# The first batch's values: maximum and halves a pass sooner, all 25 pieces placed ahead of the first turned probabilities

## The chip, the core and the metric

The kernel runs on one core of a Trainium2 chip. The metric is the time of one execution on the device in microseconds (us), smaller is better. The core has five engines that work side by side and each through its own list of instructions, in order: TensorE (PE in the rows; PEld is its loading of weights), VectorE (DVE), ScalarE (ACT), GpSimd (POOL) and SyncE (SP, which here only issues transfers). An engine that waits for a semaphore holds up all that stands behind the wait in its list.

## The reference

A transformer block on x of 4 batches of 2048 tokens, 512 wide:

```python
x = x + cross_attention(layernorm(x), ctx_768)       # 16 heads of 32, 77 keys per batch
x = x + moe_ffn(layernorm(x))                        # 8 experts, top 2, capacity 1024 tokens
```

Of the attention, what matters here is the side of the values, of each batch b:

```python
v = (key_value @ Wv + bv)                            # 77 rows of 512, for each of 4 batches
attn = softmax(clip(q @ k.T * scale, -1e4, 1e4))
o = einsum('bhqk,bhkd->bqhd', attn, v)
x = x + o @ Wo + bo
```

Products are made in halves: a float32 number is scaled by a power of two taken from the largest magnitude of its tensor, and cut into two float16 numbers, high and low, and three products of halves stand for one of float32.

## The kernel before

The 8192 tokens are 64 tiles of 128; two tiles are a group. A pass h of the main loop works on many tiles at once, each engine at another step of another tile. The loop begins at h = -7; what comes before it in the code sets up keys, values and weights. The order in each engine's list is written out by hand. In pass h:

- TensorE: `o_mm(h)` (out projection, lines 1094 and 1099), `tx(h+11)` (turns the normed tile, 1002), half of `q_mm` (queries of a group, 1029), `pv_mm` (probabilities by values, 1080), `s_mm(h+7)` (scores, 1052), `t2(h)`, the other half of `q_mm`.
- VectorE: `s_sum(h+5)` (1464) and `s_recip`, `residual(h)` (1486), `tx_lo(h+11)` (1430), the statistics of the tiles that `stats_at(h)` names (1317, 1319), and `score(h+7)`: maximum, limit and difference (1435, 1441, 1447).
- ScalarE: `ln1_apply(h+12)` (706), `s_min(h+6)` (737), `tx_hi(h+11)` (716), `s_exp(h+6)` (745), `r_scale(h+5)` (750), `q_hi` (729, 732), `o_hi`, `p_hi(h+5)` (760).
- POOL: `p_norm(h+5)` (542), `q_lo` (524), `o_lo` (530), `p_lo(h+5)` (548), and small steps of the norms in between. `all_max(n, order)` (567) is a reduce over all partitions; it waits until `order` maxima have been made.
- SP: `p_T(h+4)` (the turned copy of the probabilities, 381), `load_x(h+14)` into one of 3 buffers xt (344), `load_s` of the tiles that VectorE's statistics take in the next pass, into one of 2 buffers xs (356; it waits until the statistics two tiles before are made), stores, and from pass -2 on two placed pieces of a later batch.

The values of all four batches are made in float32 (`vf`, 77 partitions). Their maximum is reduced on VectorE (line 1867) and on POOL (`all_max(2, 4)`), a scale comes of it on VectorE (`scale_of`, lines 1362 to 1371), ScalarE makes the high half (line 899) and VectorE the low half (line 1848), into `vsh`. The product needs them elsewhere: heads lie 77 rows apart and not on chunks of 128, so `values_place(b, k)` (line 391) copies them in 25 pieces a batch into `vb`, each a transfer of its own from SP, of 1 to 77 rows with 64 bytes. `pv_mm` of a batch's first group waits for all 25, and for the turned probabilities of its two tiles.

Before the change, the values' maximum stands at the end of pass -7 on VectorE, `all_max(2, 4)` in pass -6 on POOL, the scale in -6, the high half in -6 behind `q_hi`, the low half in -5, and the pieces in passes -5, -4 and -3 of SP (9, 9 and 7), each time behind that pass's turned probabilities and loads. The same scale step of `wo` (`scale_of(3, ...)`) goes side by side with that of the values.

Of the kernel before, what the change touches and what calls it, by code (L numbers as in the profile page):

```python
# [69 lines left out]
def steps(gen, n):  # L70
    for _ in range(n):
        next(gen, None)


def alternate(*gens):
    gens = list(gens)
    while gens:
        for gen in list(gens):
            try:
                next(gen)  # L80
            except StopIteration:
                gens.remove(gen)
# [3 lines left out]
def xattn_moe(nc, x, ctxT, wq, bq, wk, bk, wv, bv, wo, bo, embT, w1T, w2T, out, xrow):  # L86
    ctx = ExitStack()
    with ctx:
# [250 lines left out]
        def sync(sp):  # L339
# [34 lines left out]
            def p_T(t):  # L374
                if not 0 <= t < T:
                    return
                G, j = divmod(t, TG)
                if G >= 2:
                    sp.wait_ge(S["pv"], 2 * (G - 1))
                sp.wait_ge(S["plo"], t + 1)  # L380
                sp.dma_start_transpose(pT[:, G % 2].rearrange("p a c n -> p (a c) n")[:, :, j * P:(j + 1) * P],
                                       ph[:, t % 2].rearrange("p a n -> p (a n)")).then_inc(S[f"pT{t % 2}"], 16)
# [52 lines left out]
                sp.dma_start(wof[DH * j:DH * (j + 1), :, :], wo_j[j]).then_inc(S["l_wo"], 16)  # L435

            for h in range(-7, T):
                p_T(h + 4)
                if h + 14 >= RT + XT:
                    load_x(h + 14)  # L440
                if h >= 1:
                    load_r(h + 4)
                for t in stats_at(h + 1):
                    load_s(t)
                if -5 <= h < -2:
                    for k in range(9 * (h + 5), 9 * (h + 6)):
                        values_place(0, k)
                if h == -2:
                    sp.wait_ge(S["made"], 5)
                    sp.wait_ge(S["bor"], 1)  # L450
                    for i in range(3):
                        sp.dma_start(bo3[i:i + 1, :], bot[0:1, i, :]).then_inc(S["l_b3"], 16)
                store_x(h)
                store_o(h)
                b, beat = (h + 18) // 16, (h + 18) % 16
                if 1 <= b < B:
                    values_place(b, 2 * beat)
                    values_place(b, 2 * beat + 1)
                if h == 50:
                    load_w(0, 1)  # L460
                if h == 56:
                    load_w(0, 2)
                if h in (22, 38, 54):
                    store_s((h - 22) // 16)
# [12 lines left out]
        def gpsimd(pool):  # L477
# [145 lines left out]
            for h in range(-7, T):  # L623
                G, half = divmod(h, 2)
                Q, part = divmod(h + 9, 2)
                if h == -7:
                    all_max(3, 3)
                if h == -6:
                    all_max(2, 4)
                if h == -3:  # L630
                    bias_rows()
                for b in range(2, len(XB)):
                    if h == seed_at(b) + 1:
                        first = norm_pool(b)
                if h == -5:
                    steps(first, 99)
                if h in (16, 32, 48, 61):
                    second = norm2_pool({16: 0, 32: 1, 48: 2, 61: 3}[h])
                if h == 61:
                    steps(second, 99)  # L640
                p_norm(h + 5)
                steps(first, 4)
                steps(second, 2)
                q_lo(Q, 2 * part)
                steps(first, 3)
                o_lo(G + 1, half)
                q_lo(Q, 2 * part + 1)
                steps(first, 9)
                steps(second, 2)
                p_lo(h + 5)  # L650
# [24 lines left out]
        def scalar(act):  # L675
# [71 lines left out]
            def r_scale(t):  # L747
                if 0 <= t < T:
                    act.wait_ge(S["r"], t + 1)
                    act.activation(rr[:, t % 2, :], rr[:, t % 2, :], ACT.Copy, scale=PSC).then_inc(S["rs"], 1)  # L750
# [131 lines left out]
            for h in range(-7, TAIL):  # L882
                G, half = divmod(h, 2)
                Q, part = divmod(h + 9, 2)
                for H in ones_at(h):
                    ones = onehot(H)
                ln1_apply(h + 12)
                s_min(h + 6)
                tx_hi(h + 11)
                if h in (20, 36, 52):  # L890
                    second_exp((h - 20) // 16)
                s_exp(h + 6)
                steps(ones, 1)
                r_scale(h + 5)
                q_hi(Q, 2 * part)
                if h == -6:
                    act.wait_ge(S["scale"], 4)
                    act.wait_ge(S["lo"], 1)
                    act.activation(flat3(vsh[0:NKV, 0]), flat3(vf[0:NKV, :, :]), ACT.Copy, scale=sv[0:NKV]
                                   ).then_inc(S["hi"], 1)  # L900
                if h == -4:
                    act.wait_ge(S["scale"], 4)
                    act.activation(flat3(woh[:, 0]), flat3(wof[:, :, :]), ACT.Copy, scale=so).then_inc(S["hi"], 1)
                o_hi(G + 1, half)
                t2_copy(h)
                q_hi(Q, 2 * part + 1)
                steps(ones, 1)
                p_hi(h + 5)
# [389 lines left out]
        def vector(dve):  # L1298
# [510 lines left out]
            dve.wait_ge(S["l_wo"], 80)  # L1809
            abs_max(3, flat3(wof[:, :, :])).then_inc(S["amax"], 1)  # L1810
            tx_lo(3)
            route = iter(())
            weights = iter(())

            for h in range(-7, TAIL):
                H = inverted_at(h)
                if h in (16, 32, 48):
                    route = routing({16: 0, 32: 1, 48: 2}[h])
                    steps(route, 1)
                if h in (20, 36, 52):  # L1820
                    route = choice((h - 20) // 16)
                if h in (22, 38, 54):
                    route = ranking((h - 22) // 16)
                    steps(route, 1)
                s_sum(h + 5, 0)
                residual(h)
                if H:
                    add_slots(H)
                s_sum(h + 5, 1)
                for g in ones_at(h):  # L1830
                    value(g)
                if H:
                    next_batch(H[-1])
                steps(route, 4)
                s_recip(h + 5)
                tx_lo(h + 11)
                ln2_stats(h)
                ln2_aggr(h)
                for t in stats_at(h):
                    ln1_stats(t)  # L1840
                for b in range(2, len(XB)):
                    if h == seed_at(b):
                        steps(norm1(b), 9)
                if h == -6:
                    alternate(scale_of(3, 5, 3, 2.0 ** -50), scale_of(2, 4, 4, 2.0 ** -50))
                if h == -5:
                    dve.wait_ge(S["hi"], 3)
                    dve.scalar_tensor_tensor(flat3(vsh[0:NKV, 1]), flat3(vf[0:NKV, :, :]), sv[0:NKV],
                                             flat3(vsh[0:NKV, 0]), ALU.mult, ALU.subtract).then_inc(S["lo"], 1)
                    dve.wait_ge(S["early"], 8)  # L1850
                    dve.tensor_scalar(embm[:, :], bM[:, 0:E], -1.0 / D, None, ALU.mult).then_inc(S["embc"], 1)
                    dve.wait_ge(S["embc"], 1)
                    dve.tensor_tensor(embc[:, :, :], embs[:, :, :], embm[:, :].unsqueeze(1).to_broadcast([P, 4, E]),
                                      ALU.add).then_inc(S["embc"], 1)
                if h == -4:
                    dve.tensor_scalar(co, isv, iso, 1.0 / PSC, ALU.mult, ALU.mult).then_inc(S["fact"], 1)
                    bias_scaled()
                if h == -3:
                    dve.wait_ge(S["hi"], 4)
                    dve.scalar_tensor_tensor(flat3(woh[:, 1]), flat3(wof[:, :, :]), so, flat3(woh[:, 0]), ALU.mult,  # L1860
                                             ALU.subtract).then_inc(S["lo"], 1)
                if h in (19, 21, 23, 35, 37, 39, 51, 53, 55):
                    steps(route, 99)
                score(h + 7)
                if h == -7:
                    dve.wait_ge(S["kvf"], 8)
                    dve.tensor_reduce(scr[0:NKV, 2:3], flat3(vf[0:NKV, :, :]), AX_X, ALU.max,
                                      apply_absolute_value=True).then_inc(S["amax"], 1)

            for h in range(TAIL, T):  # L1870
                H = inverted_at(h)
# [156 lines left out]
```

## Time and profile before

| | us |
|---|---|
| median of 3 runs | 1442.85 |
| lowest, highest | 1439.77, 1443.17 |
| the profiled execution | 1441.63 |
| its span | 1439.9 |

Shares of the span in which the engines were busy: TensorE 91%, VectorE 66%, ScalarE 56%, POOL 50%. The attention's passes fill the span until about 780 us, the experts the rest. A row of a timeline gives the start in us, the length in us, engine, line, operation, out<-in, the shape, a count where several alike are merged, and in brackets how long the engine stood idle before it and what ended that. A length can overlap the next start by about 0.1 us. "issue" in the brackets is idle time for which the profile shows no one waited for.

### The profile page before, as it was taken

To read this page: it belongs to the slowest core of one execution; us is meant where nothing else is said; L and a number is where in the kernel's file an instruction comes from. 1 tells how busy PE (TensorE), PEld (TensorE's weight loads), DVE (VectorE), ACT (ScalarE), POOL (GpSimd) and SP (SyncE) were. 2 spreads that over 40 slices of the span, in tenths; PEclk is the share of its full clock that TensorE was granted. 3 is DMA by queue.
4 is the path that set the end of the run, shared out by engine and by line. 5 is a ranking of instruction groups with operands and counts; after the bars stand their busy time and mean duration, and the time that the engine had idled before them with its cause. 6 is when DMAs were issued, how large, how long until landed. Compare 5 with 4: busy or idle time off the path is not lost.

```text
span 1439.9 us, 30591 instructions
## 1 busy us (share of the span) xinstructions
PE 1315.5 (91%) x12330; PEld 775.1 (54%) x12330; DVE 955.1 (66%) x1808; ACT 812.6 (56%) x1336; POOL 715.2 (50%) x717
## 2 busy tenths in 40 slices
PE   6458999989998999997849999999999999999996
PEld 3336777767676677764527444444444444444442
DVE  8678898889889787887775545444554545455421
ACT  4558888878998899987455514233251514334210
POOL 3187878777777678876423232242514223241301
PEclk9869999999999999999869999999999999999998
DMA  6147898978887786788433564565546455654401
GB/s 197 52 94 197 205 251 211 230 188 192 204 219 171 181 182 168 183 220 202 132 102 111 168 177 146 154 177 133 163 124 180 141 151 168 156 138 123 105 15 44
DMA packets 319575, 228.89 MB, mean 159 GB/s; under 512 B 253305, under 2 KB 253689, under 8 KB 319434
## 3 DMA queue, kind: packets, MB, share of 16 engines
q1 hardware_dynamic: 304074, 176.28, 49.4%
q0 software_dynamic: 15360, 50.66, 11.9%
q8 instruction: 97, 1.59, 0.4%
q14 instruction: 44, 0.36, 0.1%
HBM read 118.98 MB, written 50.86 MB: 118 GB/s over the span
## 4 chain that ended last, share of the span: by engine, by line
PE 72%; DVE 12%; POOL 7%; issue 4%; ACT 2%; SPq 2%; DMA 1%; DVEq 0%; POOLq 0%; ACTq 0%
PE ps L1213 23%; PE ps L1199 23%; PE ps L1099 8%; PE ps L1029 7%; PE ps L1080 3%; PE ps L1116 2%; POOL sd L542 2%; PE ps L1013 2%; PE ps L1052 1%; DVE x L1486 1%; POOL qT L524 1%; DVE sm L1464 1%; POOL ph L548 1%; PE ps L1002 1%; POOL oT L530 1%
## 5 line engine op out<-in xcount | busy, mean ns | idle before, releaser
L1199 PE MATMUL ps<-xT,w1s 128*128 128x512 f16 (+1 forms) x1632 | 336.5, 369 | 1.9 <-DVE xT L1729 1.5
L1213 PE MATMUL ps<-w2s,hT 128*128 128x512 f16 x1536 | 332.8, 379 | 0.0
L849 ACT ACTIVATE hT<-ps 128x512 f16<-128x512 f32 (+1 forms) x136 | 77.8, 572 | 356.0 <-PE ps L1199 356.0
L1199 PEld LDWEIGHTS ps<-xT,w1s 128*128 128x128 f16 x1632 | 160.6, 99 | 175.5 <-issue 1.9
L1213 PEld LDWEIGHTS ps<-w2s,hT 128*128 128x128 f16 x1536 | 150.2, 98 | 181.3
L593 POOL DMA_INDIRECT out_dram<-ys,idx x64 | 71.4, 1116 | 278.7 <-DVE ys L1769 274.5
L542 POOL TENSOR_TENSOR sd<-sd,rr 128x1232 f32<-128x1232 f32 x64 | 143.9, 2248 | 117.0 <-ACT rr L750 116.9
L1029 PE MATMUL ps<-xnT,wqh 128*128 128x256 f16 x1536 | 194.3, 278 | 5.7 <-ACT partq L732 5.5
L1099 PE MATMUL ps<-woh,oT 128*128 128x512 f16 x768 | 180.2, 384 | 3.7 <-POOL oT L530 3.7
L1759 DVE SCALAR_TENSOR_TENSOR hT<-ps,hT 128x512 f16<-128x512 f32 (+1 forms) x136 | 88.6, 658 | 138.5 <-ACT hT L849 138.4
L1769 DVE SCALAR_TENSOR_TENSOR ys<-ps,gs,og 128x512 f32<-128x512 f32 x64 | 48.1, 751 | 189.7 <-PE ps L1213 189.7
L548 POOL TENSOR_TENSOR ph<-sd,ph 128x1232 f16<-128x1232 f32 x64 | 162.2, 2534 | 12.2 <-ACT ph L760 11.4
L1029 PEld LDWEIGHTS ps<-xnT,wqh 128*128 128x128 f16 x1536 | 150.6, 99 | 28.9 <-ACT partq L732 6.3
L1099 PEld LDWEIGHTS ps<-woh,oT 128*128 128x128 f16 x768 | 75.2, 99 | 91.3 <-POOL oT L530 6.9
L1080 PE MATMUL ps<-pT,vb 128*32 128x256 f16 (+1 forms) x2400 | 89.0, 283 | 22.2 <-DMA vb<-vsh 11.0
L524 POOL TENSOR_TENSOR qT<-partq,qT 128x256 f16<-128x256 f32 x128 | 87.9, 688 | 35.9 <-ACT partq L732 20.7
L1447 DVE SCALAR_TENSOR_TENSOR sd<-ps,lim,mx 128x1232 f32<-128x1232 f32 x64 | 96.0, 1501 | 6.4
L1464 DVE TENSOR_REDUCE sm<-sd 128x8 f32<-128x616 f32 x128 | 99.5, 783 | 0.0
L1435 DVE TENSOR_REDUCE ps<-ps 128x16 f32<-128x1232 f32 x64 | 91.2, 1425 | 7.2 <-PE ps L1052 7.2
L1486 DVE SCALAR_TENSOR_TENSOR x<-ps,scr,xr 128x512 f32<-128x512 f32 x64 | 48.0, 750 | 66.8 <-PE ps L1099 66.6
L579 POOL DMA_INDIRECT xg<-xrow_dram,gix x64 | 65.6, 1025 | 48.6 <-DVE gix L1677 28.6
L1080 PEld LDWEIGHTS ps<-pT,vb 128*32 128x32 f16 (+1 forms) x2400 | 67.1, 98 | 39.2 <-issue 35.6
(206 smaller groups left out, 2012.4 us busy)
## 6 DMA issues: line engine op xcount, KB each, us to landing
xr<-x SPq DMA_DIRECT2D x64, 256.0 KB, 3.6
xrow_dram<-x SPq DMA_DIRECT2D x64, 256.0 KB, 3.7
out_dram<-x SPq DMA_DIRECT2D x64, 256.0 KB, 4.2
stage<-w1T SPq DMA_DIRECT2D x8, 2048.0 KB, 9.5
stage<-w2T SPq DMA_DIRECT2D x8, 2048.0 KB, 8.4
xt<-x SPq DMA_DIRECT2D x59, 256.0 KB, 3.2
xs<-x SPq DMA_DIRECT2D x56, 256.0 KB, 4.2
wqf<-wq SPq DMA_DIRECT2D x1, 1024.0 KB, 7.8
```

Of the source, the lines that this page charges most:

```text
L524: pool.tensor_tensor(qT[:, G % 2, 1, g, :], partq[:, g % 2, :], qT[:, G % 2, 0, g, :], ALU.subtract).then_inc(S["qlo"], 1)
L542: pool.tensor_tensor(heads(t), heads(t), rr[:, t % 2, :].unsqueeze(2).to_broadcast([P, HEADS, NKV]), ALU.mult).then_inc(S["pn"], 1)
L548: pool.tensor_tensor(ph[:, t % 2, 1, 0:KALL], sd[:, t % SDB, :], ph[:, t % 2, 0, 0:KALL], ALU.subtract).then_inc(S["plo"], 1)
L1029: ins = pe.matmul(bA[n][:, 0:GW], wqh[:, b, k, g * P:(g + 1) * P], xnT[:, G % 2, 4 * a + k, :], start=(k == 0 and i == 0), stop=(k == 3 an ...
L1080: ins = pe.matmul(bA[n][strip, cols], vb[0:K, b, a, k, strip], pT[0:K, G % 2, d, c, :], start=(i == begins[j]), stop=(i == ends[j]), tile_ ...
L1099: ins = pe.matmul(bA[0][:, :], oT[:, G % 2, a, g, j * P:(j + 1) * P], woh[:, b, g, :], start=False, stop=(g == 3 and i == 2))
L1199: ins = pe.matmul(hb[z][:, 0:wide], w1s[e % 2][:, a, k, ic * P:(ic + 1) * P], xT[:, 4 * b + k, cols], start=(k == 0 and i == 0), stop=(k = ...
L1213: ins = pe.matmul(yb[z][:, :], hT[:, a, k, s * P:(s + 1) * P], w2s[e % 2][:, b, k, :], start=(k == 0 and i == 0), stop=(k == 7 and i == 2))
L1435: dve.tensor_reduce(four(raw), scores, AX_X, ALU.max).then_inc(S["raw"], 1)
L1447: dve.scalar_tensor_tensor(sd[:, t % SDB, :].rearrange("p (g j k) -> p g j k", g=4, j=4), scores, lim[:, 2:3], four(mx[:, t % 2, :]).unsqu ...
L1464: dve.tensor_reduce(sm[:, t % 2, hs], heads(t)[:, hs, :], AX_X, ALU.add).then_inc(S["sm"], 1)
L1759: dve.scalar_tensor_tensor(hT[:, 1, ic, cols], hb[(f - 1) % 4][:, 0:count * P], 0.0, hT[:, 0, ic, cols], ALU.max, ALU.subtract).then_inc(S ...
```

## The change

- VectorE: the maximum of `vf` is made before the loop, right behind `tx_lo(3)`. The two scales are made at the end of pass -7 and not in pass -6, the low half in pass -6 and not in -5.
- POOL: `all_max(2, 4)` stands in pass -7, right behind `all_max(3, 3)`.
- ScalarE: the high half, in pass -6 as before, stands ahead of `r_scale` and the first `q_hi` of the pass.
- SP: all 25 pieces of batch 0 are issued at the start of pass -5, ahead of that pass's loads and of the first turned probabilities.

```diff
             for h in range(-7, T):
+                if h == -5:
+                    for k in range(len(pieces)):
+                        values_place(0, k)
                 p_T(h + 4)
...
-                if -5 <= h < -2:
-                    for k in range(9 * (h + 5), 9 * (h + 6)):
-                        values_place(0, k)
...
                 if h == -7:
                     all_max(3, 3)
-                if h == -6:
                     all_max(2, 4)
...
                 s_exp(h + 6)
-                steps(ones, 1)
-                r_scale(h + 5)
-                q_hi(Q, 2 * part)
                 if h == -6:
                     act.wait_ge(S["scale"], 4)
                     act.wait_ge(S["lo"], 1)
                     act.activation(flat3(vsh[0:NKV, 0]), flat3(vf[0:NKV, :, :]), ACT.Copy, scale=sv[0:NKV]
                                    ).then_inc(S["hi"], 1)
+                steps(ones, 1)
+                r_scale(h + 5)
+                q_hi(Q, 2 * part)
...
             tx_lo(3)
+            dve.wait_ge(S["kvf"], 8)
+            dve.tensor_reduce(scr[0:NKV, 2:3], flat3(vf[0:NKV, :, :]), AX_X, ALU.max,
+                              apply_absolute_value=True).then_inc(S["amax"], 1)
...
                 if h == -6:
-                    alternate(scale_of(3, 5, 3, 2.0 ** -50), scale_of(2, 4, 4, 2.0 ** -50))
-                if h == -5:
                     dve.wait_ge(S["hi"], 3)
                     dve.scalar_tensor_tensor(flat3(vsh[0:NKV, 1]), flat3(vf[0:NKV, :, :]), sv[0:NKV],
                                              flat3(vsh[0:NKV, 0]), ALU.mult, ALU.subtract).then_inc(S["lo"], 1)
+                if h == -5:
                     dve.wait_ge(S["early"], 8)
...
                 if h == -7:
-                    dve.wait_ge(S["kvf"], 8)
-                    dve.tensor_reduce(scr[0:NKV, 2:3], flat3(vf[0:NKV, :, :]), AX_X, ALU.max,
-                                      apply_absolute_value=True).then_inc(S["amax"], 1)
+                    alternate(scale_of(3, 5, 3, 2.0 ** -50), scale_of(2, 4, 4, 2.0 ** -50))
```

SP's list at the first piece (the two rows ahead are `load_x(8)` and `load_s(12)`), the difference between before and the change:

```order
 L344 DMA xt<-x 128x512
 L356 DMA xs<-x 128x512
-L344 DMA xt<-x 128x512
-L356 DMA xs<-x 128x512 x2
 L391 DMA vb<-vsh 77x2x32
 L391 DMA vb<-vsh 51x2x32
```

Gone from here are `load_x(9)` and `load_s(13)`, `load_s(14)`. They stand behind the last piece, where the same list goes on:

```order
 L391 DMA vb<-vsh 3x2x32
 L391 DMA vb<-vsh 77x2x32
+L344 DMA xt<-x 128x512
+L356 DMA xs<-x 128x512 x2
+L381 DMA_TRANSPOSE pT<-ph 128x20x128
+L344 DMA xt<-x 128x512
+L356 DMA xs<-x 128x512
```

The first row with a plus is `load_x(9)`, the second `load_s(13)` and `load_s(14)`, the third `p_T(0)`; before, the last two stood ahead of the tenth piece at the latest.

POOL's list in passes -7 and -6, before (a row "ISA" without operands is a change of the code that POOL runs, ahead of a reduce over partitions and behind it):

```order
L567 ISA
L567 ISA scr<-scr 128x1 [waits amax]
L524 ISA
L524 TENSOR_TENSOR qT<-partq,qT 128x256 [waits qf] x2
```

and then the same four rows again. With the change the two passes together are:

```order
L567 ISA
L567 ISA scr<-scr 128x1 [waits amax] x2
L524 ISA
L524 TENSOR_TENSOR qT<-partq,qT 128x256 [waits qf] x4
L486 TENSOR_SCALAR mv_96<-mv_96 128x4 [waits seed1]
```

Both reduces stand in one row, and one pair of changes of the code is gone.

VectorE's list from the values' scale to the low half (line 1848), before:

```order
L1371 RECIPROCAL scr<-scr 128x1 [waits v] x2
L1435 TENSOR_REDUCE ps<-ps 128x16 [waits s]
L1441 TENSOR_SCALAR mx<-ps,lim 128x16 [waits raw]
L1447 SCALAR_TENSOR_TENSOR sd<-ps,lim,mx 128x1232 [waits mx]
L1464 TENSOR_REDUCE sm<-sd 128x8 [waits e]
L1464 TENSOR_REDUCE sm<-sd 128x8
L1472 RECIPROCAL rr<-sm 128x16 [waits sm]
L1430 TENSOR_TENSOR xnT<-ps,xnT 128x4x128 [waits xTh]
L1317 BN_STATS st_94<-xs 128x6 [waits l_s0]
L1319 BN_AGGR mv_96<-st_94 128x2 [waits lns]
L1848 SCALAR_TENSOR_TENSOR vsh<-vf,scr,vsh 77x2048 [waits hi]
```

and with the change (lines of its list are one lower in most places):

```order
L1370 RECIPROCAL scr<-scr 128x1 [waits v] x2
L1429 TENSOR_TENSOR xnT<-ps,xnT 128x4x128 [waits xTh]
L1316 BN_STATS st_94<-xs 128x6 [waits l_s0]
L1318 BN_AGGR mv_96<-st_94 128x2 [waits lns]
L1316 BN_STATS st_94<-xs 128x6 [waits l_s1]
L1318 BN_AGGR mv_96<-st_94 128x2 [waits lns]
L1340 TENSOR_SCALAR nw<-mv_96 128x4 [waits lna]
L1343 TENSOR_SCALAR mv_96<-nw 128x4 [waits v]
L1346 TENSOR_SCALAR mv_96<-mv_96 128x4 [waits v]
L1848 SCALAR_TENSOR_TENSOR vsh<-vf,scr,vsh 77x2048 [waits hi]
```

`score(1)` and the sum of tile 0 no longer stand between them; the statistics of tiles 10 and 11 do.

## Rows read from the trace of the kernel before

**Rows 1.** Busy time by stretch: engines in us, granted clock, DMA share, GB/s.

```profile
120.00:780.00 660.00, 599.31 (x8573) 435.53 (x8574) 550.97 (x1173) 535.42 (x934) 460.10 (x434) 0.96 0.76 188
```

**Rows 2.** A piece of the chain that ended last, then TensorE's timeline.

```profile
103.20 2.02 DMA vb<-vsh
...
105.46 2.12 PE L1080 MATMUL ps<-pT,vb 128*32 128x256 f16 x36 [10.96 <-DMA vb<-vsh]
...
120.00 1.47 PE L1099 MATMUL ps<-woh,oT 128*128 128x512 f16 x6 [0.56 <-POOL oT L530]
```

**Rows 3.** VectorE's timeline, passes -7 to -1.

```profile
46.72 0.69 DVE L1430 TENSOR_TENSOR xnT<-ps,xnT 128x512 f16<-128x512 f32 x1 [1.47 <-ACT xnT L716]
...
48.94 1.42 DVE L1435 TENSOR_REDUCE ps<-ps 128x16 f32<-128x1232 f32 x1
...
52.21 2.27 DVE L1867 TENSOR_REDUCE scr<-vf 77x1 f32<-77x2048 f32 x1
...
60.26 0.15 DVE L1362 TENSOR_SCALAR scr<-scr 128x1 int32<-128x1 int32 x1 [2.91 <-POOL scr L567]
...
61.34 1.43 DVE L1435 TENSOR_REDUCE ps<-ps 128x16 f32<-128x1232 f32 x1
...
67.93 2.32 DVE L1848 SCALAR_TENSOR_TENSOR vsh<-vf,scr,vsh 77x2048 f16<-77x2048 f32 x1
...
81.86 0.68 DVE L1317 BATCH_NORM_STATS2 st<-xs 128x6 f32<-128x512 f32 x1
...
85.08 1.43 DVE L1435 TENSOR_REDUCE ps<-ps 128x16 f32<-128x1232 f32 x1
...
92.31 1.00 DVE L1347 TENSOR_SCALAR mv<-mv 128x4 int32<-128x4 int32 x1
...
95.49 1.44 DVE L1435 TENSOR_REDUCE ps<-ps 128x16 f32<-128x1232 f32 x1
...
108.53 1.45 DVE L1435 TENSOR_REDUCE ps<-ps 128x16 f32<-128x1232 f32 x1 [4.34 <-PE ps L1052]
```

**Rows 4.** POOL's timeline, passes -6 and -2 to -1.

```profile
59.85 0.38 POOL L567 PARTITION_ALL_REDUCE scr<-scr  x1 [6.06 <-issue]
68.06 2.71 POOL L524 TENSOR_TENSOR qT<-partq,qT 128x256 f16<-128x256 f32 x1 [7.83 <-issue]
...
103.26 2.25 POOL L542 TENSOR_TENSOR sd<-sd,rr 128x1232 f32<-128x1232 f32 x1 [1.12 <-ACT rr L750]
...
108.88 1.16 POOL L530 TENSOR_TENSOR oT<-parto,oT 128x512 f16<-128x512 f32 x1 [0.99 <-ACT parto L775]
111.00 0.68 POOL L524 TENSOR_TENSOR qT<-partq,qT 128x256 f16<-128x256 f32 x1 [0.97 <-ACT partq L732]
```

**Rows 5.** ScalarE's timeline, passes -6 and -2.

```profile
53.92 1.32 ACT L745 ACTIVATE sd<-sd,lim 128x1232 f32<-128x1232 f32 x1
...
61.46 2.00 ACT L899 ACTIVATE vsh<-vf,scr 77x2048 f16<-77x2048 f32 x1 [5.48 <-DVE scr L1371]
...
100.17 1.21 ACT L737 ACTIVATE sd<-sd 128x1232 f32<-128x1232 f32 x1
...
102.98 0.20 ACT L750 ACTIVATE rr<-rr 128x16 f32<-128x16 f32 x1
```

**Rows 6.** The DMA queue's timeline; last, line 391 from 70 to 79 (ns min/median/max).

```profile
56.56 11.60 SPq L356 DMA_DIRECT2D xs<-x  x2
70.34 7.78 SPq L391 DMA_DIRECT2D vb<-vsh  x9
...
98.23 5.85 SPq L391 DMA_DIRECT2D vb<-vsh  x7
...
L391 SPq DMA_DIRECT2D vb<-vsh x9: 639/847/1033, 70.3 to 77.2; - x9
```

**Rows 7.** Loads of xs, issue to landing: from 47 to 50, from 85 to 99.

```profile
DMA to landing us min/median/max: 4.4/4.4/4.4
...
DMA to landing us min/median/max: 3.0/3.3/3.6
```

## The prediction, made before the changed kernel was timed

> **What bounds the kernel now.** I began with the stretches [rows 1]: from 120 us on TensorE is busy 599 of 660 us. The change touches only the start before that, so what it can give is a shift of the start, and it can give it once: where the engines come together again at about 120 us, everything behind runs as before. Next I read the chain and TensorE's rows about the first batch's values [rows 2]. The last of the 25 pieces is issued at 103.20 and lands 2.02 later; TensorE has then stood idle 10.96 us in front of `pv_mm(0,0)` (line 1080), that is from 94.50 to 105.46. This is the wait that the change goes for. But at 120.00 the second half of `o_mm(0)` waits for something else, POOL's `o_lo` (line 530). So I read POOL back from there, VectorE, ScalarE and the DMA queue, to see what else stands at pass 0 when the values are early.
>
> **The sum, part by part.** Times are those of the profiled execution.
>
> 1. *Maximum sooner.* `tx_lo(3)` is over at 45.2, since VectorE then waits 1.47 until `tx_lo(4)` at 46.72. The reduce of `vf` fills this wait: 45.2 and 2.2, as before (2.27 with its tail) [rows 3]. Its result is there at 47.4 and not at 54.5. What is pushed back is `tx_lo(4)`, from 46.72 to 47.4, and with it two statistics and `score(0)`, from 48.94 to 49.6. It takes 3.27 (48.94 to 52.21) and ends at 52.85.
>
> 2. *POOL.* Going from ordinary work to a partition reduce costs 6.06 us of idle time before it (the row of 59.85), and going back cost 7.83 (the row of 68.06) [rows 4]. Before, `all_max(2)` stands behind `q_lo`, pays this, and gives its result at 60.26, where VectorE waited 2.91 for it. Now it stands right behind `all_max(3)`; the maximum of 47.4 gives the result before 49. One change there and back is gone: about 14 us of POOL. `q_lo(1,0)` starts at about 56 (under 49 and 7.83), and nobody asks for it before `s_mm(2)`, which waits for scores until past 60.
>
> 3. *Scale and halves.* The scale's eight small instructions start when `score(0)` is done, 52.85, and take 1.1 (60.26 to 61.34 in the trace, where `score(1)` follows): 54.0. ScalarE first does `s_min(0)` and the turned copy and `s_exp(0)`, the last at 53.92 plus 0.65, until 55.8; the first half of the values takes 1.9 (2.00 with its tail) [rows 5] and ends at 57.8. VectorE's second half (line 1848, 67.93, 2.32 with its tail) now runs from 57.85 to 60.1. So the halves are ready 10.1 us sooner than the 70.2 of before.
>
> 4. *Placing.* The 16 pieces of the two timed stretches took 7.78 and 5.85 us, 0.852 each; 25 take 21.3 us: 60.3 to 81.6 [rows 6]. With 2.02 for landing the values are in place at 83.6 instead of 105.22. TensorE's order lets `pv_mm(0,0)` start when what stands ahead of it is done (below: 98.0), so this wait of 10.96 is gone entirely.
>
> 5. *What is queued behind the 25.* SP works in order. `load_x(9)` and `load_s(13)`, `load_s(14)` were issued from 56.56 on, the last at 67.8, ahead of the placing. Now they come behind it: 81.6, 82.2, 82.6. A load of xs lands 3.0, 3.3 or 3.6 us after issue in the rows of 85 to 99 and 4.4 in those of 47 to 50 [rows 7]; I take 3.3, the median of the rows nearest in place. Tile 13 is there at 85.5, tile 14 at 85.9 (bounds 85.2 and 87.0). VectorE needs tile 13 in pass -4. In the trace that is at 81.86. With the halves 10.1 sooner it comes there at 73 to 78: between line 1848 and the statistics lay 11.7 us (70.2 to 81.86), and `score(1)` and `s_sum(0)`, 6.6 us (61.34 to 67.93), have moved behind line 1848: 60.1 + 18.3 = 78.4 at the latest, 73 if the 4 to 5 us of waiting for ScalarE in the trace go. So VectorE stands 7 to 12 us before tile 13, where it stood for nothing before. From 85.5 on: `score(3)` 3.2 later (81.86 to 85.08): 88.7 against 85.08, **3.5 us later than before**. `score(4)`: 95.49 + 3.5 = 99.0, done at 102.3 [rows 3].
>
> 6. *TensorE.* `s_mm(4)` waits for `score(3)`'s end, 92.0 (88.4 before). From there to the start of the idle time at 94.50 lay 6.1 us: `pv_mm(0,0)` starts at 98.0, 7.5 us sooner than 105.46. `s_mm(5)` behind it waits for 102.3. VectorE without the wait of 4.34 before `score(5)` would have come there at 104.2; plus 3.5 is 107.7, against 108.53 before: no longer held by TensorE, and 0.8 ahead.
>
> 7. *POOL at pass -2 to 0.* `p_norm(3)` started at 103.26, released by ScalarE's `r_scale` [rows 4, 5]. ScalarE takes 3.0 us from `s_min(4)` (100.17) to the end of `r_scale` (103.18). Before, it began 1.3 after the score was done, being busy; now it is free, so 102.3 + 3.0 + 0.1 = 105.4: POOL starts that row 2.1 later. From there to `o_lo(0,1)` POOL has no free time but two waits, 0.99 (the row of 108.88) and 0.97 (the row of 111.00), both for ScalarE's copies of what TensorE made late. TensorE is early now, so they go: 2.1 - 2.0 = +0.1. With 0.1 for rounding, `o_mm(0)`'s second half starts at 120.2 instead of 120.00. From there on the order is the same on all engines.
>
> Sum: about +0.2 us. The profiled execution took 1441.63 (span 1439.9), the median of the runs is 1442.85. So that execution would take 1441.8, the median 1443.05; I say 1443.1.
>
> The row of 92.31 shows a small VectorE instruction (line 1347, 4 elements) lasting 1.00 us, where the one of 60.26 takes 0.15 [rows 3], and the `q_lo` of 68.06 lasts 2.71 against the 0.68 of 111.00, while line 1848 runs [rows 4]. The Trainium skill, page "SBUF — State Buffer", section "Who interferes with whom", has the rule for it: VectorE and GpSimd share one port pair, and whichever takes it first holds it for the whole instruction. This speaks against the change: line 1347 shifted by 3.5 falls at 95.8, inside `p_norm(2)`, which I get at 95.1 to 97.3, so it would be held until 97.3 where a plain shift gives 96.8. By that rule the sum is +0.7, without it +0.2.
>
> **Unknown costs.** The 25 in a row: the trace has nine in a row at most. The two stretches had 0.864 and 0.836 each (+0.3, -0.4); the single ones go from 0.639 to 1.033 [rows 6], which if all were so would be -5.3 and +4.5. I stay by the stretches and keep +4.5 for a rival; below, -5.3 would be cut off where ScalarE and TensorE set the pace, at 2 to 3. Landing -0.3 to +1.1. Small waits between VectorE and POOL in the shifted stretch, the 0.85 too much in the row of 92.31: -0.8 to +0.6. How much of POOL's two waits goes: 0 to 2.0, so 0 to +2.0.
>
> **Rivals.**
> *A, the gain comes through.* If pass 0 were set by TensorE's backlog and not by POOL, the 7.5 us of `pv_mm(0,0)` would be kept: 1442.85 - 7.5 = 1435.3. For it: the wait is on the chain, and 10.96 is the longest single one of TensorE there. Against: the chain leaves TensorE for POOL at 111.00 and the row of 120.00 names POOL [rows 2, 4]; POOL's input hangs on VectorE, and that on tile 13. I give 0.13. A part of it (1438.5 to 1441) would look like no change.
> *B, slower, the queue of SP.* The 25 issues in a row go slower than nine, or the loads behind them land late. Place: SP between 60.3 and 86; the price goes one to one into tile 13 and, as all slack of POOL's is used up, into the end. At 1.033 each and 4.4 for landing: 4.5 + 1.1 + 0.2 = +5.8, 1448.7. It decides from a mean issue of 1.02 us on (+4.2). For it: issue is by SP, and one of 25 reached 1.03. Against: nine in a row took no more each than seven did, within 0.03. I give 0.13.
> *C, the change does not do what it says.* If the halves were held by ScalarE or by POOL's change back, the placing would begin near 70 as before, with the loads behind it: tile 13 at 95, over 9 us later, 1452. The order leaves no room for it, since the reduce stands directly behind its like; 0.03.
>
> **How the numbers follow.** The forecast has 0.71. Three runs of before lie between 1439.77 and 1443.17, so under 0.3% (4.3 us, 1438.5 to 1447.2) is no change that can be told. The forecast's own range by the unknown costs is 1440 to 1447. For 8 in 10 the range is 1438 to 1447.5: it leaves most of A and C and the upper end of B out. Faster: A with the tail of the forecast, 0.16. Slower: most of B, C and a tail, 0.18. Same: 0.66.
>
> **What would show it.** In the trace after: the `vf` reduce near 45; the partition reduce at about 48 with no idle time of 6 us of its own; line 1848 near 58; 25 pieces from 60 to 82 in one row; VectorE idle 7 to 12 us for a DMA of xs before the statistics at about 85.5 (the main step: if there is none, A holds); no wait for vb at `pv_mm`, which starts near 98; `p_norm(3)` near 105.4 with no waits behind it, and `o_mm(0)`'s second half at 120.2 behind POOL. I am wrong if the statistics of tile 13 run before 80, or if `o_mm(0)` is not released by POOL.

## The result and the profile after

The changed kernel takes 1445.24 us at the median of 22 runs (1441.93 to 1449.37), the kernel before 1443.15 in as many runs (1439.77 to 1445.99). The ratio is 1.0016, 95% interval 1.0009 to 1.0024. So it is 2.1 us slower: the interval leaves out 1, and the whole of it is within the 0.3% that the prediction set for "no change". The profiled execution took 1443.62 (span 1441.8, granted clock 0.963); that of before 1441.63 (1439.9, 0.966).

The DMA queue's timeline after shows the 25 pieces as one row, and the loads of xt and xs (tiles 13 and 14) that came ahead of them before now behind it:

```profile
60.74 21.18 SPq L391 DMA_DIRECT2D vb<-vsh  x25
81.97 0.51 SPq L344 DMA_DIRECT2D xt<-x  x1
82.53 0.90 SPq L356 DMA_DIRECT2D xs<-x  x2
83.47 4.54 SPq L381 DMA_TRANSPOSE pT<-ph  x1
```

TensorE's timeline after. The wait of 10.96 us for the values [rows 2] is gone and `pv_mm(0,0)` starts 7.3 us sooner. Ahead of it `s_mm(4)` starts 3.6 us later than before (88.50). Behind it `s_mm(5)` starts 3.2 us sooner (107.51 before), but waits 4.99 for VectorE's `score(4)`. The second half of `o_mm(0)` waits longer for POOL (1.85 for 0.56) and starts 2.06 us later than the 120.00 of [rows 2]:

```profile
92.07 0.97 PE L1051 MATMUL ps<-kb,qT 32*128 32x77 f16 x48 [14.10 <-DVE sd L1446]
98.13 1.18 PE L1079 MATMUL ps<-pT,vb 128*32 128x256 f16 x36
104.29 0.97 PE L1051 MATMUL ps<-kb,qT 32*128 32x77 f16 x48 [4.99 <-DVE sd L1446]
...
122.06 1.47 PE L1098 MATMUL ps<-woh,oT 128*128 128x512 f16 x6 [1.85 <-POOL oT L530]
```

VectorE's timeline after. First read the wait of 10.65 us before the statistics of tile 13 at 85.64, which stood for nothing before; then the three small instructions of 4 elements at 95.40, 97.46 and 98.09, which last 2.03, 0.60 and 0.59 us; then the distance between the two `score` reduces (line 1434), 88.65 and 100.87. It is 12.22 us; in [rows 3] it was 10.41 (85.08 to 95.49):

```profile
45.67 2.27 DVE L1812 TENSOR_REDUCE scr<-vf 77x1 f32<-77x2048 f32 x1
...
58.30 2.35 DVE L1848 SCALAR_TENSOR_TENSOR vsh<-vf,scr,vsh 77x2048 f16<-77x2048 f32 x1 [0.20 <-ACT vsh L895]
...
85.64 0.69 DVE L1316 BATCH_NORM_STATS2 st<-xs 128x6 f32<-128x512 f32 x1 [10.65 <-DMA xs<-x]
...
88.65 1.43 DVE L1434 TENSOR_REDUCE ps<-ps 128x16 f32<-128x1232 f32 x1
...
95.40 2.03 DVE L1340 TENSOR_SCALAR nw<-mv 128x4 f32<-128x4 f32 x1
97.46 0.60 DVE L1343 TENSOR_SCALAR mv<-nw 128x4 int32<-128x4 int32 x1
98.09 0.59 DVE L1346 TENSOR_SCALAR mv<-mv 128x4 int32<-128x4 int32 x1
...
100.87 1.43 DVE L1434 TENSOR_REDUCE ps<-ps 128x16 f32<-128x1232 f32 x1
```

POOL's timeline after. At 45.83 and 48.04 the two partition reduces stand together: only the first waits some 6 us, the second starts 0.1 us after its input (the `vf` reduce ends at 47.94). The stretch from 95 on shows what VectorE's small instructions ran beside, and `p_norm(3)` at 107.37, 4.1 us later than in [rows 4]:

```profile
45.83 0.38 POOL L567 PARTITION_ALL_REDUCE scr<-scr  x1 [6.32 <-issue]
48.04 0.35 POOL L567 PARTITION_ALL_REDUCE scr<-scr  x1 [1.84 <-DVE scr L1812]
56.03 1.29 POOL L524 TENSOR_TENSOR qT<-partq,qT 128x256 f16<-128x256 f32 x2 [7.64 <-issue]
...
95.16 2.25 POOL L542 TENSOR_TENSOR sd<-sd,rr 128x1232 f32<-128x1232 f32 x1 [1.99 <-ACT rr L749]
97.36 1.30 POOL L524 TENSOR_TENSOR qT<-partq,qT 128x256 f16<-128x256 f32 x2
98.79 4.53 POOL L548 TENSOR_TENSOR ph<-sd,ph 128x1232 f16<-128x1232 f32 x1
107.37 2.25 POOL L542 TENSOR_TENSOR sd<-sd,rr 128x1232 f32<-128x1232 f32 x1 [4.06 <-ACT rr L749]
```

The chain that ended last leads from the load of tile 14 over these instructions of VectorE and ScalarE to POOL and from there to the second half of `o_mm(0)`. No transfer of values is in it any more:

```profile
82.99 4.07 DMA xs<-x
...
95.40 2.04 DVE nw L1340
...
107.37 2.25 POOL sd L542
...
122.06 1.47 PE ps L1098 x6
```

### The profile page after: what moved, and what is told of

Its sections match the earlier page's. It is cut to its first block, busy times and chain, and to the rows that moved or that the text cites. A ratio compares the mean times of both kernels' runs of the same rounds, so it can differ in the third digit from the quotient of the medians.

```text
span 1441.8 us, 30524 instructions
## 1 busy us (share of the span) xinstructions
PE 1315.3 (91%) x12267; PEld 779.0 (54%) x12330; DVE 957.3 (66%) x1808; ACT 812.3 (56%) x1336; POOL 714.2 (50%) x717
## 4 chain that ended last, share of the span: by engine, by line
PE 72%; DVE 13%; POOL 6%; issue 3%; ACT 3%; SPq 2%; DMA 1%; DVEq 0%; POOLq 0%; ACTq 0%
PE ps L1212 23%; PE ps L1198 23%; PE ps L1098 9%; PE ps L1028 6%; PE ps L1079 3%; PE ps L1115 2%; POOL sd L542 2%; PE ps L1012 2%; SPq L391 1%; DVE sm L1463 1%; DVE x L1485 1%; PE ps L1051 1%; DVE ps L1434 1%; PE ps L1001 1%; POOL oT L530 1%
## 5 line engine op out<-in xcount | busy, mean ns | idle before, releaser
L1028 PE MATMUL ps<-xnT,wqh 128*128 128x256 f16 x1536 | 199.5, 282 | 8.5 <-ACT partq L731 8.2
L1079 PE MATMUL ps<-pT,vb 128*32 128x256 f16 (+1 forms) x2400 | 88.0, 280 | 11.3 <-issue 3.8
L736 ACT ACTIVATE sd<-sd 128x1232 f32<-128x1232 f32 x64 | 78.5, 1226 | 29.8 <-DVE sd L1446 29.6
```

What stands on the lines that cost most here:

```text
L1028: ins = pe.matmul(bA[n][:, 0:GW], wqh[:, b, k, g * P:(g + 1) * P], xnT[:, G % 2, 4 * a + k, :], start=(k == 0 and i == 0), stop=(k == 3 an ...
L1079: ins = pe.matmul(bA[n][strip, cols], vb[0:K, b, a, k, strip], pT[0:K, G % 2, d, c, :], start=(i == begins[j]), stop=(i == ends[j]), tile_ ...
```

## The experiments

The theory after the first comparison, for the changed kernel: the gain at `pv_mm(0,0)` is real, but pass 0 no longer hangs on it; pass 0 is set by POOL, POOL by the scores, and the scores by the loads of tiles 13 and 14 behind the 25 pieces; 1.8 us more come from VectorE and POOL holding each other at 95 to 101. The rivals: the row of 25 itself costs or gains on its own (whatever the order of VectorE and POOL); or the earlier maximum is worth nothing anyway. Seven kernels were run in two sets, each set beside the kernel before (medians 1442.75 and 1442.69).

**1. The changed kernel with the loads inside the row** (8 pieces, loads of pass -5, 17 pieces):

```diff
                 if h == -5:
-                    for k in range(len(pieces)):
+                    for k in range(8):
                         values_place(0, k)
                 p_T(h + 4)
...
                 for t in stats_at(h + 1):
                     load_s(t)
+                if h == -5:
+                    for k in range(8, len(pieces)):
+                        values_place(0, k)
```

> As the changed kernel, but the loads of pass -5 (tile 9 for ScalarE, tiles 13 and 14 for VectorE) stand between the eighth and the ninth of the 25 pieces. My theory (what the row of pieces bought is lost since VectorE waits for loads queued behind it): the wait of 10.65 us before the statistics of tile 13 goes, they start near 75. But the load of tile 15 stands behind the rest of the pieces and the first turned probabilities, near 89, so VectorE waits for tile 15 until about 92, against 94.39 now: score(4) comes 2.5 to 4 us sooner (97 to 98.4 instead of 100.87), the second half of o_mm(0) likewise at 118 to 119.5 instead of 122.06, and the whole takes 0.997 to 0.999 of before. Rival (the end is held by POOL's port lock or by something else and not by the loads): no wait at tile 13, but o_mm(0) stays at 122 and the time at 1.0016 of before.

Measured: 1440.32, ratio 0.9984 (0.997 to 0.9999), as expected: 2.4 us under its own kernel before, where the changed kernel is 2.1 over, so 4.5 us by moving three loads. VectorE's timeline of this kernel: tile 13 waits no longer, but tile 15 does, since its load (pass -4) is still behind the 17. The wait has moved one tile on, as the expectation said:

```profile
74.60 0.68 DVE L1319 BATCH_NORM_STATS2 st<-xs 128x6 f32<-128x512 f32 x1
...
90.85 0.69 DVE L1319 BATCH_NORM_STATS2 st<-xs 128x6 f32<-128x512 f32 x1 [7.20 <-DMA xs<-x]
91.86 0.94 DVE L1343 TENSOR_SCALAR nw<-mv 128x4 f32<-128x4 f32 x1
...
95.38 1.45 DVE L1437 TENSOR_REDUCE ps<-ps 128x16 f32<-128x1232 f32 x1
```

The small instruction at 91.86 lasts 0.94 instead of 2.03, and `score(4)` comes at 95.38, 5.5 us sooner than after and 1.6 sooner than expected. The second half of `o_mm(0)` starts at 116.59, again 5.5 us sooner (118 to 119.5 expected). The rival, that the end does not hang on the loads, falls.

**2. The row alone** (the kernel before, its halves late as they were, all 25 pieces at the start of pass -5):

```diff
+                if h == -5:
+                    for k in range(len(pieces)):
+                        values_place(0, k)
                 p_T(h + 4)
...
-                if -5 <= h < -2:
-                    for k in range(9 * (h + 5), 9 * (h + 6)):
-                        values_place(0, k)
```

> The kernel before with one part of the change alone: all 25 pieces in one row at the start of pass -5, maximum and halves where they were. My theory: pieces 70.3 to 91.6, tile 13 there at about 95.5, score(3) 13.6 us later than before, o_mm(0)'s second half at 130 to 132 instead of 120.0, the whole 1.007 to 1.0085 of before. Rival (early placing by itself is good, since TensorE's wait of 10.96 for the values goes): values in place at 93.6 instead of 105.2 and the whole 0.995 of before.

Measured: 1454.0, 1.008 (1.006 to 1.01), within the expected 1.007 to 1.0085; the rival's 0.995 falls. The queue and VectorE of this kernel (in its profiled execution the first piece already stood 2.8 us later than in that of before, 73.17 for 70.34, and what lies ahead of it likewise):

```profile
73.17 21.19 SPq L391 DMA_DIRECT2D vb<-vsh  x25
```

```profile
98.00 0.69 DVE L1317 BATCH_NORM_STATS2 st<-xs 128x6 f32<-128x512 f32 x1 [13.86 <-DMA xs<-x]
```

The row of 25 took 21.2 us here as in the changed kernel, and the loads behind it were issued that much later. The second half of `o_mm(0)` starts at 134.36; less the 2.8 that is 131.6, within the expected 130 to 132. The three small instructions behind tile 15's statistics last 2.03, 0.59 and 0.60 here too, so the second cost of the changed kernel comes with the row and not with the early halves.

**3. The early halves alone** (the changed kernel's engines, the pieces 9, 9 and 7 behind the loads as before):

```diff
-                if h == -5:
-                    for k in range(len(pieces)):
-                        values_place(0, k)
                 p_T(h + 4)
...
+                if -5 <= h < -2:
+                    for k in range(9 * (h + 5), 9 * (h + 6)):
+                        values_place(0, k)
```

> The changed kernel with the other part alone: maximum and halves a pass sooner, the pieces 9, 9 and 7 behind the loads of passes -5, -4 and -3 as before. My theory: no wait of VectorE for a load; pieces from 67.5, the last one issued at 97 and landed at about 100; pv_mm(0,0) starts at 100 instead of 105.46 (98.13 in the changed kernel), score(5) at about 103 instead of 108.53, and the second half of o_mm(0) at 114.5 instead of 120.0: 5.5 us faster, 0.996 of before. Rival (pass 0 hangs on POOL or the early halves bring nothing): 0.999 to 1.001 of before.

Measured: 1435.87, 0.9954 (0.9936 to 0.9972), as expected. This half of the change alone is worth -6.9 us, and the other half takes it back and 2.1 more. TensorE of this kernel still waits 10.32 us for the values, nearly as long as before, but `pv_mm(0,0)` starts 6.5 us sooner than before, and pass 0 is 6.0 us sooner:

```profile
98.95 2.11 PE L1079 MATMUL ps<-pT,vb 128*32 128x256 f16 x36 [10.32 <-DMA vb<-vsh]
...
113.98 1.47 PE L1098 MATMUL ps<-woh,oT 128*128 128x512 f16 x6 [0.56 <-POOL oT L530]
```

Its `score(4)` is at 88.36 (95.49 before), with no wait for a load ahead of it. Beside the changed kernel this shows what sets pass 0 there: `pv_mm(0,0)` starts within 0.8 us of the same place in both (98.95 and 98.13), and pass 0 lies 8.1 us apart (113.98 and 122.06), as POOL's `p_norm(3)` does by more (96.12 and 107.37).

The wait for the values is not free in this kernel, though. Here, as before the change, the chain that ended last runs through the last piece and `pv_mm(0,0)`, and POOL waits for what TensorE made late:

```profile
96.12 2.25 POOL L542 TENSOR_TENSOR sd<-sd,rr 128x1232 f32<-128x1232 f32 x1 [1.12 <-ACT rr L749]
...
102.36 1.15 POOL L530 TENSOR_TENSOR oT<-parto,oT 128x512 f16<-128x512 f32 x1 [1.61 <-ACT parto L774]
104.99 0.67 POOL L524 TENSOR_TENSOR qT<-partq,qT 128x256 f16<-128x256 f32 x1 [1.47 <-ACT partq L731]
```

The two waits are 3.1 us, against 2.0 before [rows 4]. That, and not 10.32, is the price of the wait at pass 0; experiment 5 takes it away.

**4. The changed kernel, in pass -3 both `q_lo` ahead of `p_norm(2)` on POOL**, so that no small instruction of VectorE meets a long one of POOL:

```diff
+                if h == -3:
+                    q_lo(Q, 2 * part)
+                    q_lo(Q, 2 * part + 1)
...
-                q_lo(Q, 2 * part)
+                if h != -3:
+                    q_lo(Q, 2 * part)
...
-                q_lo(Q, 2 * part + 1)
+                if h != -3:
+                    q_lo(Q, 2 * part + 1)
```

> As the changed kernel, but in pass -3 POOL makes both q_lo before p_norm(2) and not after it. It tells what made the 2.03 us of VectorE's 4-element instruction (line 1340) at 95.40, and with it the 1.9 us by which score(4) came later than my sum had it. Port lock (p_norm(2) of 95.16 to 97.41 holds VectorE off): lines 1340, 1343 and 1346 take some 0.2 to 0.7 each, line 1861 starts near 96.2 and holds POOL off in turn, score(4) starts near 98.4 instead of 100.87; p_norm(3) at 105.5 instead of 107.37, the whole about 1.8 us faster than the changed kernel, 1.0004 of before. Rival (the length comes from elsewhere, clock or record): line 1340 stays near 2 us, score(4) at 100.9, and the time stays 1.0016 of before or above.

Measured: 1442.73, 0.9999 (0.9987 to 1.0011), where 1.0004 was expected. VectorE's timeline of this kernel has the small instructions at 0.17 us each, and `score(4)` 2.3 us sooner:

```profile
95.35 0.17 DVE L1345 TENSOR_SCALAR nw<-mv 128x4 f32<-128x4 f32 x1
95.56 0.17 DVE L1348 TENSOR_SCALAR mv<-nw 128x4 int32<-128x4 int32 x1
95.84 2.82 DVE L1866 SCALAR_TENSOR_TENSOR woh<-wof,scr,woh 128x2048 f16<-128x2048 f32 x1
98.58 1.44 DVE L1439 TENSOR_REDUCE ps<-ps 128x16 f32<-128x1232 f32 x1
```

The same place on POOL: now POOL pays, its two `q_lo` take 3.35 us beside the instruction of 95.84, where they took 1.30:

```profile
95.84 3.35 POOL L524 TENSOR_TENSOR qT<-partq,qT 128x256 f16<-128x256 f32 x2 [2.72 <-ACT partq L736]
99.15 2.24 POOL L542 TENSOR_TENSOR sd<-sd,rr 128x1232 f32<-128x1232 f32 x1
...
106.41 2.25 POOL L542 TENSOR_TENSOR sd<-sd,rr 128x1232 f32<-128x1232 f32 x1 [1.12 <-ACT rr L754]
```

`p_norm(3)` comes at 106.41, not at the expected 105.5: `p_norm(2)` moved back four us, ScalarE waited 4.94 for it at 101.48, and so came late to `s_min(4)`. The second half of `o_mm(0)` starts at 121.11, 0.95 sooner than after (1.8 expected). The signature of the hold came as forecast, and the rival (a length that comes from the clock or the record) falls. The gain at pass 0 came only by half. At the median the kernel gains more, 0.0 over its kernel before against the changed kernel's +2.1 and +2.2; where the rest of that comes from no trace shows.

**5. The loads of both passes in time** (8 pieces, loads, 5 pieces; in pass -4 the turned copy of `p_T(0)`, loads, 12 pieces):

```diff
                 if h == -5:
-                    for k in range(len(pieces)):
+                    for k in range(8):
                         values_place(0, k)
...
+                if h == -5:
+                    for k in range(8, 13):
+                        values_place(0, k)
+                if h == -4:
+                    for k in range(13, len(pieces)):
+                        values_place(0, k)
```

> As the changed kernel, but every load of x stands where VectorE finds it in time: in pass -5 eight pieces, that pass's loads, five pieces; in pass -4 the turned probabilities of tile 0, the loads of tiles 10 and 15, then the other twelve pieces. My theory: no wait of VectorE for a load, score(4) at 88.4 as with the early halves alone, second turned probabilities issued at about 87.6 and landed at 92.6, pv_mm(0,0) starts there (98.95 with the early halves alone), score(5) at 97.1 by VectorE's own work, second half of o_mm(0) at 111 against 120.0 in the kernel before and 114.0 with the early halves alone: 9 us faster than before, 0.993 to 0.9945. Rival (the early placing gives nothing beyond the early halves, since the passes behind are set elsewhere): 0.9954 as the kernel with the early halves alone.

Measured: 1436.93, 0.9957 (0.9941 to 0.9974), worse than the expected 0.993 to 0.9945, and the number that the rival gave (0.9954, nothing gained beyond the early halves). But the start came as expected: no wait for xs, `score(4)` at 88.55, and TensorE at pass 0 nine us sooner:

```profile
93.18 2.11 PE L1085 MATMUL ps<-pT,vb 128*32 128x256 f16 x36 [4.91 <-DMA pT<-ph]
...
111.01 1.47 PE L1104 MATMUL ps<-woh,oT 128*128 128x512 f16 x6 [0.18 <-POOL oT L536]
```

Its `p_norm(3)` stands at 96.32, where experiment 3 has it (96.12), and POOL's two waits are gone. Pass 0 comes 3.0 us sooner than there, which is those two waits. So in the trace the rival falls; at the median this run cannot tell, and experiment 6 does.

**6. All 25 ahead of `p_T(0)`, the loads of both passes inside the row** (after the 8th and after the 17th piece):

```diff
-                    for k in range(len(pieces)):
+                    for k in range(8):
                         values_place(0, k)
                 p_T(h + 4)
-                if h + 14 >= RT + XT:
+                if h + 14 >= RT + XT and h != -4:
                     load_x(h + 14)
...
-                for t in stats_at(h + 1):
-                    load_s(t)
+                if h != -4:
+                    for t in stats_at(h + 1):
+                        load_s(t)
+                if h == -5:
+                    for k in range(8, 17):
+                        values_place(0, k)
+                    load_x(10)
+                    load_s(15)
+                    for k in range(17, len(pieces)):
+                        values_place(0, k)
```

> As the changed kernel, all 25 pieces ahead of the first turned probabilities, but the loads of passes -5 and -4 (tiles 9, 13, 14 and 10, 15) stand between them, behind the eighth and the seventeenth piece. If only the loads behind the row cost, and not the turned probabilities behind it, it is as fast as the version with the loads on time: pv_mm(0,0) at 92 to 94, o_mm(0)'s second half at 110 to 112, 0.993 to 0.995 of before. If the delay of the turned probabilities costs too, the second ones land after 95 and o_mm(0) comes after 113, 0.995 or more.

Measured: 1432.95 (1432.25 to 1433.66), 0.9927 (0.9913 to 0.9942), just under the expected 0.993 to 0.995. It beats both kernels: 9.7 us under the kernel before. Its queue, then TensorE: the 25 pieces are still there, 21.2 us of issue in three parts of 8, 9 and 8 with the loads between them, and VectorE waits for no load of xs. The turned probabilities stand behind all of it, and `pv_mm(0,0)` at 92.49 and `o_mm(0)` at 110.72 are within the ranges for the case that their delay costs nothing.

```profile
60.45 6.83 SPq L391 DMA_DIRECT2D vb<-vsh  x8
...
68.72 7.71 SPq L391 DMA_DIRECT2D vb<-vsh  x9
...
77.50 6.66 SPq L391 DMA_DIRECT2D vb<-vsh  x8
84.21 6.42 SPq L381 DMA_TRANSPOSE pT<-ph  x2
```

```profile
92.49 2.11 PE L1087 MATMUL ps<-pT,vb 128*32 128x256 f16 x36 [3.96 <-issue]
...
110.72 1.47 PE L1106 MATMUL ps<-woh,oT 128*128 128x512 f16 x6 [0.18 <-POOL oT L538]
```

**7. The changed kernel again**, in the second set:

> The changed kernel again, beside the others on one chip: 1.0009 to 1.0024 of before as already measured, which lets the others be set against it run for run.

Measured: 1444.93, 1.0014 (1.0002 to 1.0025): the +2 us is there again, on another chip than that of the first set.

**How far the start carries.** The prediction and experiments 1 to 6 rest on the shift at the start being what the end shows. The starts of the first matmul of `o_mm(h)` (line 1094 before) in each of the 64 passes were read from the traces; the table gives them less those of before, in us. In pass 0 it stands ahead of the first half of `o_mm(0)`; the second half, with POOL's wait in it, shows the shift that goes on: +1.8 in the row of (7), where the column pass 0 has +0.48. The last column is the difference of the medians.

```
                          pass 0   pass 1   pass 18  pass 34  last    median
after (7)                 +0.48    +1.79    +1.85    +1.77    +1.65   +2.2
loads within (1)          -4.71    -3.41    -3.38    -1.61    -2.46   -2.4
row alone (2)            +13.07   +14.36   +14.35   +17.28   +17.05  +11.3
early halves alone (3)    -6.02    -6.02    -6.01    -5.89    -8.98   -6.9
POOL's order (4)          -0.20    +1.11    +0.62    +0.66    +0.65    0.0
loads in time (5)        -10.03    -8.99    -8.78    -8.67    -8.35   -5.8
row, loads within (6)    -10.02    -9.28    -9.29    -9.20    -9.09   -9.7
```

From pass 1 to 18 a shift moves by half a us at most, and to the end by 0.8 at most, but for jumps of 1.7 to 3.1 us at passes 19 to 21 and 35 to 37. There the granted clock differs between executions. The stretches of before, then of experiment 3, in which they pass the same place (time, TensorE, its loads, VectorE, ScalarE and POOL busy, granted clock, DMA share, GB/s):

```profile
460.00:470.00 10.00, 6.54 (x117) 5.46 (x116) 8.10 (x12) 5.37 (x13) 8.25 (x14) 0.86 0.42 79
470.00:480.00 10.00, 9.91 (x131) 6.17 (x132) 5.58 (x15) 7.51 (x15) 4.62 (x3) 0.80 0.77 203
```

```profile
450.00:460.00 10.00, 6.78 (x119) 4.56 (x118) 7.70 (x12) 6.24 (x11) 7.85 (x20) 1.00 0.28 97
460.00:470.00 10.00, 9.66 (x144) 7.11 (x145) 8.59 (x18) 9.71 (x20) 7.77 (x6) 1.00 0.86 204
```

Both have the thin stretch in which TensorE is busy 6.5 to 6.8 of 10 us; before was granted 0.86 there and 0.80 behind it, between the two levels of 1.2 and 2.4 GHz, and experiment 3 the full 2.4 in both, and gained 3.1 us there. So of the -9.0 with which its trace ends, 6.0 come from the start. What decides the clock was not found. The same holds for 4 us that part experiments 5 and 6 at the median (1436.93 and 1432.95): their profiled executions took 1434.0 and 1432.94 and show the same start. Of the six runs of experiment 5 three lie at 1434.0 to 1435.7 and three at 1438.1 to 1438.6, 3 us apart, the size of one such jump; only one was profiled, so the cause is open.

## Why the prediction was right where it was right, and the step that was off

The forecast of no change (under 0.3%) is right, and in the main for the reason given: the 7.3 us gained at `pv_mm(0,0)` are lost again at POOL by way of tile 13. The amount is not: +0.2 was forecast and +2.1 measured, which still lies under the 4.3 us that the prediction called no change. Its row, "VectorE idle 7 to 12 us for a DMA of xs before the statistics at about 85.5", came as 10.65 us and 85.64. By its own steps:

- *Steps 1 and 2, maximum and POOL.* The `vf` reduce at 45.67 for 45.2, of which 0.5 is this execution's later start; the second partition reduce at 48.04 without the wait of 6 us; `q_lo(1,0)` at 56.03 for 56. Right.
- *Step 3, halves.* Line 1848 at 58.30 for 57.85. Right, with the same 0.5.
- *Step 4, placing.* 25 pieces in 21.18 us for 21.3, from 60.74 for 60.3. With it rival B falls in its main term: its mean of 1.02 us was 0.85.
- *Step 5, the loads.* Issued at 81.97 and 82.53 for 81.6 and 82.2; tile 13 right. Tile 14 took 4.07 us to land, not 3.3, and was there at 87.06, just past the bound of 87.0, so VectorE waited another 0.54 for it. That `score(3)` still stands at 88.65 for 88.7 is luck: the instruction on line 1422 took 0.47, where before it had taken 1.35 (line 1423). **Then its last sentence fails**: "`score(4)`: 95.49 + 3.5 = 99.0". It came at 100.87, 1.9 later.
- *Step 6, TensorE.* `s_mm(4)` at 92.07 for 92.0, `pv_mm(0,0)` at 98.13 for 98.0. `s_mm(5)` at 104.29 for 102.3: the 1.9 passed on. `score(5)` at 108.22 for 107.7.
- *Step 7, POOL at pass 0.* `p_norm(3)` at 107.37 for 105.4, and the two waits of 0.99 and 0.97 gone as forecast; the second half of `o_mm(0)` at 122.06 for 120.2. So pass 0 came at +2.06 for +0.2: the mechanism held, and one term of it was 1.9 too small. Behind it the shift is carried, +2.1 up to pass 19 and +1.7 at the last.
- *Rival A* ("set by TensorE's backlog") would have kept the 7.5 us. The trace after speaks against it directly: `pv_mm(0,0)` is 7.3 us sooner and pass 0 is 2.06 later, with the load of tile 14 and no transfer of values in the chain. In experiment 3 TensorE's wait does stand in the chain, and costs POOL's two waits of 3.1 us.

The mis-sized term is the distance from `score(3)` to `score(4)`, which the prediction took from before unchanged. Its size by the rows: line 1340 started at 95.40, just after `p_norm(2)` (95.16), and ended at 97.43, as `p_norm(2)` did at 97.41. In experiment 4, with POOL idle, the two behind it took 0.17 each; here 0.60 and 0.59 beside POOL's two `q_lo` (97.36). (2.03 - 0.25) + 0.43 + 0.42 = 2.6, of which the one in [rows 3] at 92.31 had already cost 0.85: 1.8 more than before. The prediction named this place. It had the rule from the Trainium skill, page "SBUF — State Buffer", section "Who interferes with whom": whichever of VectorE and GpSimd takes the shared port pair first holds it for its whole instruction. The trace agrees, with ends at 97.43 and 97.41. But the prediction reckoned +0.5 for it and left even that out of the sum, and its bounds for small waits between VectorE and POOL, -0.8 to +0.6, left the 1.8 out too. It put only the last of the three small instructions (line 1347, at 95.8) inside `p_norm(2)` (95.1 to 97.3). The first stands 0.5 ahead of it, so by the prediction's own numbers it was caught too, for nearly the whole of `p_norm(2)`, and the next two met the next POOL instructions; the prediction did not look at them. Experiment 4 shows the cause, by taking the meeting away: `score(4)` came 2.3 us sooner, though POOL then paid in turn and half of it was lost by pass 0.

The forecast "everything behind runs as before" holds to within the jumps above, which are of the size of the effect itself. In the second trace of the changed kernel none fell: +1.79 at pass 1, +1.65 at the last.

Where the gain went, then, by halves of the change: early halves alone -6.9 us (experiment 3); the row ahead of the loads alone +11.3 (experiment 2); both +2.1, since the early halves leave the row room to stand earlier. Early halves and the row with the loads inside it are worth -9.7 (experiment 6). The prediction saw the price of the queue, but not that moving five loads avoids it.

## What to carry to other kernels

- Before a row of small transfers is pulled forward, write down what stands behind it on that queue and who waits for that. Here the cost was 0.85 us a piece, 25 times, ahead of loads whose own issue takes 0.4 to 0.5 us and that VectorE needed first. Putting the loads inside the row turned +2.1 us into -9.7.
- The length of the longest wait on the busiest engine is not its price: the wait of 10 us at `pv_mm(0,0)` stood in the version that gained 6.9 us and was gone in the one that lost 2.1. Where it stood in the chain it cost what it made POOL wait, 2.0 us before and 3.1 in experiment 3. Read back from where the engines next come together.
- When a shift slides a chain of tiny VectorE instructions along POOL's timeline, lay each of the chain against each of POOL's instructions. Here a meeting cost the rest of the POOL instruction, not a share of it (2.03 beside 2.25 us), and whoever is moved out of the way may make the other pay.

## What was new of the hardware

- A second partition reduce right behind the first had neither idle time of 6 us before it nor one of 7 to 8 between the two: it started at 48.04, 0.1 us after its input, against 6.06 of idle time for the same instruction before [rows 4]. The way back was paid once, 7.64, before the instruction of 56.03.
- Instructions of 4 elements lasted 2.03, 0.60 and 0.59 us beside POOL's and 0.17 without (experiment 4); a long one of POOL (`p_lo`, line 548) lasted 4.53 beside VectorE's of 98.60 and 2.52 without it in experiment 4.
- Issue time of the small transfers did not depend on how many stood in a row: 0.847 each for 25, 0.857 for the 9 of experiment 6, 0.845 for the 17 of experiment 1. A turned copy issued right behind the loads of xs took 4.54 us in the queue, against 3.14 where pieces stood right before it (experiment 5); why was not tested.
- The granted clock in the same thin stretch of two kernels was 0.86 and 1.00, and 0.80 and 1.00 right behind it, and their executions drew 3.1 us apart there, more than the change did. Differences of this size need medians of many runs, not two traces.
